# A register loop over pairs of batches is written out as straight-line bodies

## The reference, cut to what matters

```
y  = layernorm(x)
a  = self_attention(layernorm(y)) + y             # 16 heads of 8, causal
b  = cross_attention(layernorm(a), encoder) + a   # shared keys, key bias, mask 2 wide of the diagonal
c  = b + gelu(layernorm(b) @ fc) @ mlp_proj       # 128 -> 512 -> 128
x  = x + layernorm(c)
z  = layernorm(x)
o  = shared expert(z) + sum over top 2 of 8 experts (swiglu: silu(a) * b), weighted by softmax gates
out = x + layernorm(o)
```

## Time and profile before

| | |
|---|---|
| median of 3 runs | 1765.04 us |
| the 3 runs | 1765.84, 1759.42 and 1765.04 us |
| the profiled execution's own time | 1766.79 us |
| span in its trace, first to last instruction | 1765.1 us |
| mean granted TensorE clock | 0.937 |
| busy share of the span: PE, DVE, ACT, POOL | 83%, 66%, 56%, 17% |

### The profile page before, as it was taken

One profiled execution on the slowest core, in us unless ns is written; L12 is line 12 of the kernel. 1 busy time (PEld: TensorE's weight loads), 2 busy tenths in 40 slices (PEclk: granted clock), 3 DMA queues, 4 the chain that ended last, 5 costly groups with the idle time before them and its releaser, 6 DMA issues.

```text
span 1765.1 us, 43050 instructions
## 1 busy us (share of the span) xinstructions
PE 1472.6 (83%) x16232; PEld 988.6 (56%) x16232; DVE 1163.1 (66%) x3554; ACT 982.8 (56%) x1585; POOL 308.1 (17%) x422
## 2 busy tenths in 40 slices
PE   0377888989998888988998888988898898989867
PEld 0245555655656555665656555665656566656544
DVE  5236766777767676776767666776767776737244
ACT  0143666474756657473756647474756656472632
POOL 3101121121212112121211112121211111011110
PEclk9675989999999989999999989999999999997888
DMA  3222130303021220304022220303022221010000
GB/s 82 48 44 38 27 69 18 52 9 67 9 44 27 41 36 20 56 9 68 9 37 34 41 36 16 61 9 59 18 35 35 38 33 24 11 21 13 14 6 6
DMA packets 79069, 58.30 MB, mean 33 GB/s; under 512 B 10842, under 2 KB 78740, under 8 KB 78868
## 3 DMA queue, kind: packets, MB, share of 16 engines
q1 hardware_dynamic: 75922, 54.40, 17.9%
q10 hardware_dynamic: 2946, 1.12, 0.3%
HBM read 11.57 MB, written 4.19 MB: 9 GB/s over the span
## 4 chain that ended last, share of the span: by engine, by line
PE 54%; ACT 15%; DVE 12%; issue 9%; SPq 5%; POOL 3%; DMA 1%; ACTq 0%; DVEq 0%; POOLq 0%
PE ps L1165 15%; PE ps L1190 7%; PE ps L1117 7%; DVE chunkmax L835 5%; ACT probs L621 4%; PE ps L1064 4%; PE ps L1255 3%; SPq L383 3%; PE ps L1091 3%; PE ps L1082 2%; ACT geluT L644 2%; PE ps L1154 2%; PE ps L1094 2%; ACT x_tm L599 2%; SPq L318 2%
## 5 line engine op out<-in xcount | busy, mean ns | idle before, releaser
L835 DVE TENSOR_REDUCE chunkmax<-ps 128x3 f32<-128x384 f32 (+1 forms) x1024 | 508.0, 555 | 116.2 <-PE ps L1102 110.2
L621 ACT ACTIVATE probs<-ps 128x768 f32<-128x768 f32 (+1 forms) x512 | 404.5, 809 | 190.1 <-PE ps L1097 185.3
L1165 PE MATMUL ps<-zT,w 128*128 128x512 f32 x576 | 287.1, 618 | 2.1 <-ACT silu_a L638 2.1
L638 ACT ACTIVATE silu_a<-ps,b 128x512 f32<-128x512 f32 x144 | 98.5, 684 | 220.8 <-PE ps L1165 219.7
L1190 PEld LDWEIGHTS ps<-w,hT 128*128 128x128 f32 x1152 | 154.3, 193 | 89.1 <-issue 54.4
L1082 PE MATMUL ps<-k_op,q_op 48*128 48x256 bf16 x512 | 149.4, 294 | 64.4 <-DVE chunkmax L835 45.6
L934 DVE SCALAR_TENSOR_TENSOR hT<-ps,b,silu_a 128x512 f32<-128x512 f32 x144 | 108.1, 751 | 112.4 <-PE ps L1165 77.4
L1190 PE MATMUL ps<-w,hT 128*128 128x128 f32 x1152 | 168.8, 283 | 13.4 <-DVE hT L934 13.3
L1064 PE MATMUL ps<-q_op,k_op 51*128 51x256 bf16 x512 | 141.6, 285 | 37.1 <-issue 13.7
L1082 PE MATMUL ps<-xk_op,xq_op 51*128 51x256 bf16 x512 | 148.6, 291 | 10.3 <-DVE chunkmax L835 5.8
L945 DVE SCALAR_TENSOR_TENSOR acc<-ps,gates,acc 128x128 f32<-128x128 f32 x512 | 144.1, 345 | 15.3 <-PE ps L1190 10.0
(11 more groups left out here) (217 smaller groups left out, 3462.5 us busy)
## 6 DMA issues: line engine op xcount, KB each, us to landing
q_op<-q_parts SPq DMA_DIRECT2D x192, 64.0 KB
k_op<-k_parts SPq DMA_DIRECT2D x192, 64.0 KB
xq_op<-xq_parts SPq DMA_DIRECT2D x192, 64.0 KB
x_tm<-in_L_attn_hidden_states SPq DMA_DIRECT2D x16, 256.0 KB, 5.6
x_keep<-in_L_attn_hidden_states SPq DMA_DIRECT2D x16, 256.0 KB, 5.6
out<-o_tm SPq DMA_DIRECT2D x16, 256.0 KB, 2.3
w<-in_L_ffn_rw SPq DMA_DIRECT2D x1, 1024.0 KB
q_op<-maxT SPq DMA_DIRECT2D x32, 24.0 KB
```

Of the source, the lines that this page charges most:

```text
L621: act.activation(probs[:, four % 2, 2 * pair:2 * pair + 2, 0:T + a.seen], ps[:, 2 * (g % 2):2 * (g % 2) + 2, 0:T + a.seen], ACT.Exp).then_ ...
L835: dve.tensor_reduce(chunkmax[:, b, at, :], ps[:, MAX_BANK[n], 0:3 * a.seen].rearrange("p (c n) -> p c n", c=3), AX.X, ALU.max).then_inc(a. ...
L1165: pe.matmul(ps[:, bank, :], w, src[:], start=True, stop=True).then_inc(sig.sem, 1)
```

## The change

`program` no longer makes a loop: every engine gets all 21 bodies, -2 to 18, written out, with the pair as a plain number everywhere. The order of the work in each body, the buffers, the semaphores and the tiles stay as they are. The helper that slices DRAM for a pair takes plain numbers too.

```diff
-        def program(eng, body):
-            for i in range(-2, 4):
-                body(i, i % 2)
-            with eng.Fori(4, PAIRS - 4, 2) as i:
-                body(i, 0)
-                body(i + 1, 1)
-            for i in range(PAIRS - 4, PAIRS + 3):
+        def program(body):
+            for i in range(-2, PAIRS + 3):
                 body(i, i % 2)
...
-                return x[bass.ds(sp.snap(2 * j), 2)].rearrange("b (q p) f -> p (b q) f", p=128)
+                return x[2 * j:2 * j + 2].rearrange("b (q p) f -> p (b q) f", p=128)
...
-            program(sp, body)
+            program(body)
```

More of the change, by code:

```diff
@@ L558, in body @@
                     rstd(n_mlp, tiny3, i - 1)
-            program(pool, body)
+            program(body)
         @block.scalar
@@ L736, in _ @@
             act.wait_ge(made.sem, SETUP_MADE)
-            program(act, body)
+            program(body)
         @block.vector
@@ L1016, in body @@
                     gather(k, NE)
-            program(dve, body)
+            program(body)
         @block.tensor
@@ L1333, in body @@
                     down(k, NE)
-            program(pe, body)
+            program(body)
 _INS = ['hidden_states', 'encoder_hidden_states', 'scorer_logits', 'ln1_g', 'ln1_b', 'c_attn_w', 'c_attn_b',
```

## The result

The written kernel takes 1756.41 us (median of 17 runs) and the kernel before 1765.62 in the same comparison (17 runs). The ratio is 0.9945, with a 95% interval of 0.9928 to 0.9963: 9.2 us faster by the medians and 0.55% by the ratio, where 7.6 us and 1757.4 were forecast. By the prediction's own line for "faster", 1756.2, the median stands just on the side of "same". (One of the 17 runs took 7420.58 us, far from the other 16 at 1749 to 1763, and is not in the ratio.) The profiled execution has a span of 1753.8 us, 11.3 less than before.

A forecast was written before the change was run, and what follows sets the result against it. PE, busy 83% of the span, was taken to bound the kernel. Jumps -21.8, table loads +8.8 and clock drops about +5.4 gave -7.6 us: 1765.0 to 1757.4, with an 8-in-10 range of 1748 to 1767.

The forecast's parts named there:

- line for "faster": Whole kernel: a measurement tells about 0.5%, 8.8 us, from no change, so "faster" begins below 1756.2 us; chance 0.42.
- The comparison of bodies: Bodies 4 to 11: loop bodies compared with written bodies 3, 12 and 13 in one trace; 798.0 us becomes 790.4.
- The drops: Written bodies 4 to 11: short clock drops, four bodies at 98.1 us and four at 99.5; about +5.4 us.
- the 21.8 us of the three jumps: Loop passes 2 to 4: three jumps back with all that follows cost 21.8 us, which the change removes.
- all is on the path, since PE is the engine that sets the pace: Starts of bodies 6, 8 and 10: PE's three stalls after jumps, about 13.8 us, count in full.
- 13.8 and 8.0: Split of the three jumps' 21.8 us: 13.8 us is PE's stall and 8.0 us slower clock.
- Register arithmetic: Loop bodies: register instructions computing wait numbers run while PE's array works off its queue; their removal gains nothing.
- The table loads: Written bodies: ACT's exponential load comes only after the wait for the score tile; 1.1 us per body, +8.8 in eight.
- B: Rival: clock drops fall in harmless places or not at all; gain of 13 to 15 us, 1750 to 1752; chance 0.27.
- C: Rival: all written bodies pay a clock drop like 3 and 12; gain of 2 us, 1763; chance 0.13.
- D: Rival: stalls are late code, not the jump's, and stay; table loads add 8.8 us, 1773.8; chance 0.05.
- One sign missed: Sign 4, bodies 12 and 13, outside the old loop: they were to stay as before.

The follow-up runs named there:

- experiments 1 to 3: Against the loop kernel, written out: only PE, 1765.2 us, ratio 1.0002; PE and DVE, 1743.9 us, 0.9871; only DVE, 1759.92 us, 0.9973.
- experiment 4: Against the loop kernel: all engines but PE written out, 1776.59 us, ratio 1.0053; only ACT written out, 1771.22 us, 1.0032.
- experiment 6: Fully written kernel plus tiny ACTIVATEs that load tables early: self-attention exponential 1741.92 us; with gelu 1739.74; with cross-attention too 1735.04, repeat 1731.83; cross-attention alone 1751.45.
- experiment 5: Loop kernel with its loop over bodies 3 to 12, four jumps back instead of three, and SP written out: 1766.74 us, ratio 1.0005.
- experiment 2: Loop kernel with only PE and DVE written out; SP, POOL and ACT keep the loop: 1743.9 us, ratio 0.9871.
- load 2 early: Fully written kernel with a tiny exponential ahead of the cross-attention's first exponential, the other table loads left late: 1751.45 us, ratio 0.9926 to the loop kernel.

## Why the prediction was right

**The comparison of bodies held.** Forecast for the eight bodies: 790.4 us; measured 788.7. A written body without a clock drop was put at 97.9 and took 97.8. The drops were put at 8 x 0.9 = 7.2 us and took 788.7 - 8 x 97.8 = 6.3: three bodies at 99.5 and four at 98.0 to 98.2, where four and four were assumed. That split was a guess between two levels. In the seven traces whose PE and DVE never jump, 2 to 4 of the eight bodies have the late drop, so the guess could have been off by some 3 us, and chance gave one body less. Since all engines were written out at once, the 21.8 us of the three jumps went as one sum, whatever was inside.

**The jump: right in its sum, wrong in its parts.** The step "all is on the path, since PE is the engine that sets the pace" failed as an explanation. DVE's jump costs as much (5.6 us from its last queued work to its next instruction) and runs beside PE's; experiments 1 to 3 show that PE's stall taken away alone is worth 0 us, DVE's 5, both together 18 (medians) to 23 (ratio). The prediction's account would have been 19 us off for a change that unrolled PE only. The chain of the kernel before had the row; I read only PE's branch. The split of the 21.8 us was off with it. DVE's first maximum comes 6.5, 6.7 and 7.0 us behind the start of bodies 6, 8 and 10, where it comes after 1.2 in bodies 5 and 7: 16.7 us of delay in sum and 5.1 for all that follows, not 13.8 and 8.0. The page Runtime: NRT & Kernel Launch of the Trainium skill (Instruction fetch mechanics) says that a taken branch out of the fetched window stalls its engine. PE's and DVE's stalls agree with it, each by itself; whether the jumps of POOL, SP and ACT that cost 0.2 to 0.3 us stay inside that window, no run here shows. The 108 ns of the Trainium skill's page Advanced Engine Details and Errata (Control Flow Timing) are near what the trace has where the loop is left, 83 ns in the earlier trace rows, and far from every taken jump of PE, which took 3.7, 4.0 and 6.1 us (the median of 3.8 in the earlier trace rows lies between the first two).

**Register arithmetic, priced at nothing, was mis-sized.** A body without jump and drop takes 96.8 us with PE and DVE in register form and 96.5 in written form: 0.3 us per body, some 2 us of the gain.

**The table loads: right in place and price.** All eight bodies have the exponential's load behind its wait. The price by the way to the residual add is 31.88 - 30.70 = 1.2 us (1.1 forecast), and 31.88 - 30.62 = 1.3 when the register arithmetic is kept apart. ACT's program alone brings it in (experiment 4), and moving the loads takes most of it away (experiment 6). The prediction had seen that the wait changes its place; which of the two waits stands ahead of the load, it did not ask. The Trainium skill's page ScalarE: Activation LUTs (What ACT_TABLE_LOAD costs) would have a drain of 1380 ns behind a load; after the moved load the tiny ACTIVATE starts 0.02 us behind its end (524.21 + 1.28 = 525.49, then 525.51), so there is none here either. In the kernel after, 61 of the 62 loads have the next ACTIVATE 11 or 12 ns behind them.

**The rivals.** B (1750 to 1752) would have needed the clock drops to stay in harmless places; three of eight bodies were hit. C (1763) needed all of them. D is refuted by the stalls' absence here and their move in experiment 5. A body's drop costs 1.7 us late in the body (99.5 against 97.8; 1.5 was forecast) and 0.2 to 0.3 us in its middle. What decides where it falls was not tried and stays open. One sign missed: body 13 was to be as before, 98.1, and took 99.7 us, since it has both drops.

## What to carry to other kernels

A loop's price and a straight line's price are found by comparing equal bodies of both forms in one trace; do it for every engine's jump, because stalls that run side by side hide each other: here removing one of two brought 0 or 5 us, and both 18 to 23. Before unrolling ACT's code, look whether its table loads stand ahead of a wait or behind it: here unrolling cost 1.2 us per body that way. A one-column ACTIVATE of the next function, ahead of the wait, gave 1.0 of it back, and three of them turned a gain of 0.5% into one of 1.7 to 1.8%. Where two waits precede the first use of a table, look which of them stands ahead of the load; whether swapping the two lines of code would do the same as the early load was not tried.

## What the runs showed of the hardware that was not expected

- A jump back costs each engine a different amount, and the same engine a different amount in another kernel. From the jump to the engine's next register instruction: PE 3.7, 4.1 and 6.2 us, DVE 5.9, 6.0 and 5.7, POOL 0.2, SP 0.3 and ACT 0.3 us in the kernel before. With the loop shifted by one body (experiment 5) ACT takes 4.4 to 4.5 us at each of its four jumps, where it took 0.3, and DVE 5.1 to 5.4. What decides this was not tried.
- In the kernel after, every body from 3 to 15 except body 4 has a stretch of about 3.4 us at the lower clock (1.2 GHz), at one of two places: some 37 to 39 or 76 to 77 us behind the body's start. Body 13 has both (99.7 us). Bodies of the same code differ by 1.7 us by the place of this stretch. The spread of the runs, 1749 to 1763 us, is wider than the whole gain.
- With the exponential's load behind its wait, 2 of 16 bodies are free of such a stretch (bodies 4 to 11 of the kernel after and of the one with load 2 early). With it early, 18 of 40 are (experiment 2 and the other early loads). Why was not tried.
